# Four decoder layers on one core: loads into a ninth token tile, moved value-bias products and last norm, contiguous context parts, and a new order of both halves

## The reference, cut to what matters

```python
# L0: pre-norm
h = _mha(_ln(x), _ln(x), causal=True);  x = x + h @ m_proj_w + m_proj_b      # attention 0
h = _mha(_ln(x), ctx, causal=False);    x = x + h @ c_proj_w + c_proj_b      # attention 1
x = x + relu(_ln(x) @ f_w1 + f_b1) @ f_w2 + f_b2
# L1: post-norm, mixture of experts
x = _layernorm(x + _attn(x, x, x, causal=True))                              # attention 2
x = _layernorm(x + _attn(x, ctx, ctx, causal=False))                         # attention 3
x = _layernorm(x + _moe(x))      # 8 experts (256 to 1024 to 256, gelu), the best 2 of each token
# L2: post-norm
x = _ln(x + _mha(x, x, mask));  x = _ln(x + _mha(x, ctx, None))              # attentions 4, 5
x = _ln(x + relu(x @ ff_w1 + ff_b1) @ ff_w2 + ff_b2)
# L3
y = _ln(x + softmax(Q(x) K(ctx)^T / 4) V(ctx) @ Wo)                          # attention 6
```

## Time and profile before

| | |
|---|---|
| median of 3 runs | 3065.95 us (3065.38 to 3067.84) |
| the profiled execution | 3048.22 us |
| its span, first to last instruction | 3045.8 us |
| stage a, about | 0 to 1415 us |
| stage b, about | 1415 to 1950 us |
| stage c, about | 1950 us to the end |
| mean granted TensorE clock, share of full speed | 0.964 |

### The profile page before, as it was taken

How to read it: one execution, slowest core, us unless ns; L and a number is a source line. 1 busy time by engine, 2 the same in 40 slices (tenths; PEclk the granted TensorE clock), 3 DMA queues, 4 the chain that set the end, 5 groups by cost and what they waited for, 6 DMA issues and landing times. The chain is left out here.

```text
span 3045.8 us, 58500 instructions
## 1 busy us (share of the span) xinstructions
PE 2830.4 (93%) x22574; PEld 2279.3 (75%) x22574; DVE 1681.8 (55%) x4086; ACT 1331.7 (44%) x2955; POOL 986.7 (32%) x1103
## 2 busy tenths in 40 slices
PE   6989999989999989975999999889999999999996
PEld 4768888768888777754888888656777777777774
DVE  4646556776755867554110010276676766767664
ACT  2535445556455455332222222245455545555442
POOL 2313224444323444322000000252344444444343
PEclk8999999999999999986999999899999999999997
DMA  9755546585664674754767766375466555666342
GB/s 141 119 72 67 63 54 89 84 114 75 75 71 59 90 98 72 190 74 135 241 225 231 224 211 220 87 111 63 53 85 76 80 79 75 82 77 78 43 50 40
DMA packets 393627, 317.68 MB, mean 104 GB/s; under 512 B 152155, under 2 KB 377307, under 8 KB 393339
## 3 DMA queue, kind: packets, MB, share of 16 engines
q1 hardware_dynamic: 370994, 276.25, 54.6%
q0 software_dynamic: 8272, 23.73, 2.8%
q10 hardware_dynamic: 14085, 13.97, 1.7%
HBM read 133.54 MB, written 36.57 MB: 56 GB/s over the span
## 5 line engine op out<-in xcount | busy, mean ns | idle before, releaser
L962 ACT ACTIVATE a_prob<-a_bank 128x512 f32<-128x512 f32 (+1 forms) x640 | 332.8, 603 | 146.5 <-PE a_bank L756 142.9
L1106 DVE TENSOR_REDUCE a_maxima<-a_bank 128x2 f32<-128x512 f32 (+3 forms) x576 | 339.2, 644 | 82.7 <-PE a_bank L736 82.0
L962 ACT ACTIVATE c_prob<-c_bank 128x512 f32<-128x512 f32 (+1 forms) x512 | 266.3, 599 | 194.7 <-PE c_bank L756 194.4
L989 ACT ACTIVATE b_group_hidden<-b_bank,b_b 128x256 f32<-128x256 f32 (+1 forms) x312 | 123.3, 452 | 387.7 <-PE b_bank L820 387.7
L1106 DVE TENSOR_REDUCE c_maxima<-c_bank 128x6 f32<-128x462 f32 (+1 forms) x448 | 260.4, 635 | 45.2 <-PE c_bank L736 43.9
L865 PE MATMUL a_bank<-a_causal_b,keep_identb 128*128 128x256 bf16 (+1 forms) x768 | 243.1, 316 | 29.9 <-DMA a_qs<-a_shift 12.9
L820 PE MATMUL b_bank<-b_group_xt,b_w 128*128 128x256 f32 (+1 forms) x1248 | 261.6, 364 | 6.3 <-DVE b_group_xt L1157 6.3
L802 PE MATMUL b_bank<-b_w,b_group_hidden 128*128 128x256 f32 x1136 | 251.7, 380 | 0.9 <-ACT b_group_hidden L989 0.9
L820 PEld LDWEIGHTS b_bank<-b_group_xt,b_w 128*128 128x128 f32 x1248 | 220.6, 192 | 33.7 <-DVE b_group_xt L1157 8.3
L802 PEld LDWEIGHTS b_bank<-b_w,b_group_hidden 128*128 128x128 f32 x1136 | 215.6, 190 | 29.7 <-ACT b_group_hidden L989 1.3
L1163 DVE TENSOR_TENSOR b_group_y<-b_bank,b_b 128x512 f32<-128x512 f32 (+1 forms) x39 | 25.1, 644 | 336.1 <-PE b_bank L802 336.1
(11 more groups left out here) (255 smaller groups left out, 6224.0 us busy)
## 6 DMA issues: line engine op xcount, KB each, us to landing
b_w<-in_L_xattn_e_w SPq DMA_DIRECT2D x78, 1024.0 KB, 7.4
a_qs<-a_parts_q SPq DMA_DIRECT2D x384, 128.0 KB
c_qs<-c_parts_q SPq DMA_DIRECT2D x288, 128.0 KB
a_ks<-a_parts_k SPq DMA_DIRECT2D x192, 128.0 KB, 5.9
c_ks<-c_parts_k SPq DMA_DIRECT2D x96, 128.0 KB, 5.5
sorted_in<-a_zeros SPq DMA_DIRECT2D x8, 1024.0 KB
b_group_x<-sorted_in SPq DMA_DIRECT2D x32, 256.0 KB, 6.8
sorted_out<-b_group_y ACTq DMA_DIRECT2D x32, 256.0 KB, 4.8
```

Source lines behind the costliest of these rows:

```text
L962: act.activation(prob[0:rows, first:first + cols], bank[0:rows, 0, 0:cols], ACT.Exp, scale=SCALE).then_inc(k.own(s), 1)
L989: ins = act.activation(hidden[:, f, 0:n], bank[:, 0, j * n:(j + 1) * n], ACT.Gelu, bias=b1[:, f:f + 1])
L1106: v.tensor_reduce(maxima[:, q:q + qn, h:h + n].rearrange("p q h -> p h q"), bank[:, 0, 0:cols].rearrange("p (j q n) -> p j q n", j=n, q=qn ...
```

## The change

1. `enter` in stage a loads straight into a `tok` tile, which is the residual. `loaded` goes from stage a, and `tok` has 9 tiles. GpSimd's `bias` works in place after `apply`.
2. The value-bias products of stage a stand behind a step of sequence 0: product 0 behind its value projection of attention 0, products 1, 2 and 3 behind the first `pv` of attentions 0, 1 and 2.
3. The last norm of a sequence is two VectorE steps in place: `scaled` computes (x - mean) * gain after the moments, `shifted` computes x * rstd + shift. The two GpSimd passes and the `apply` go.
4. The context's input is laid out as [sequence, 128, 2, 77], so its load has one run per partition. Its three parts are packed at the front of their tile (`parts_of`), so that a copied part is one run of 308 bytes per partition, before two of 154.
5. The planner adds 0.1 us to the start of every TensorE step that leaves the 32-column products when it compares steps. Before, the 0.1 was added only once the choice was made.
6. Both tables of `AHEAD` have new numbers.
7. The router's small steps share one semaphore.

```diff
@@ class Plan, run
-                    start = max(free_at[e], came[k])
+                    leaves = e == "tensor" and in_columns and s.kind != "pv"
+                    start = max(free_at[e] + (0.1 if leaves else 0.0), came[k])
@@ semaphore_of
+        if s.kind in ROUTING:
+            return "routing"
@@
+def last_norm_steps(plan, b, n, x, source):
+    lab = (b, n)
+    moment_steps(plan, b, n, x, source)
+    plan.step("vector", "scaled", b, n, us=0.92, after=[("moments", b, n)], x=x, moments=("moments", lab))
+    plan.step("vector", "shifted", b, n, us=0.92, after=[("scaled", b, n), ("rstd", b, n)], gives=["moments", "rstd"],
+              x=x, moments=("moments", lab), rstd=("rstd", lab))
@@ value_bias_steps
-    plan.step("tensor", "bias_out", -1, "bias", at, us=0.87, after=ready, takes=["bank"], bank=bank)
+    plan.step("tensor", "bias_out", -1, "bias", at, us=0.87, after=ready, behind=behind, takes=["bank"], bank=bank)
@@ start_steps
-                         [("fold", -1, "a")] if at == 3 else [bias_in(at)])
+                         [("fold", -1, "a")] if at == 3 else [bias_in(at)], [("value_proj" if at == 0 else "pv", 0, max(at - 1, 0), 1 if at else 0)])
@@ AHEAD, the two first lines of each half
-AHEAD = {"a": {"enters": 0.9, ("enters", "a"): -0.6, "norms": 3.3, ("norms", 0): 126.0, ("gains", 0): -19.1,
-               "turns": -0.8, ("turns", 0): 2.0, "projs": 0.8, ("projs", 0): 13.1, "values": -0.4,
...
-         "c": {"enters": 2.3, "norms": 8.4, ("norms", 4): -9.6, "turns": 1.2, ("turns", 4): -0.2, "gains": 4.7,
-               ("gains", 4): 30.5, "projs": 0.7, ("projs", 4): -0.5, "values": -0.4, ("values", 4): 1.4,
...
+AHEAD = {"a": {"enters": -89.5, ("enters", "a"): 0.8, "norms": 3.2, ("norms", 0): 0.4, "gains": 7.4,
+               ("gains", 0): -29.7, "turns": -0.9, ("turns", 0): 45.1, "projs": 0.8, "values": -0.4,
...
+         "c": {"enters": 1.0, "norms": 19.2, ("norms", 4): 62.2, "turns": 1.2, ("turns", 4): 50.9, "gains": -41.9,
+               ("gains", 4): 5.4, "projs": 1.4, ("projs", 4): -1.9, "values": -0.5, ("values", 4): 1.5,
...
@@ first_half
-    x, res = ("loaded", b), ("tok", (b, "x"))
-    plan.step("sync", "enter", b, "a", us=0.45, lag=4.0, takes=["x", "lane"], landing="x", x=x, lane=("lane", (b, "a")))
-    norm_steps(plan, b, "l0_1", x, ("tok", (b, "n0")), ("enter", b, "a"), False)
-    bias_step(plan, b, 0, x, res, ("enter", b, "a"), after=[("apply", b, "l0_1")], takes=["out"], gives=["x"])
+    res = ("tok", (b, "x"))
+    plan.step("sync", "enter", b, "a", us=0.45, lag=4.0, takes=["x", "lane"], landing="x", x=res, lane=("lane", (b, "a")))
+    norm_steps(plan, b, "l0_1", res, ("tok", (b, "n0")), ("enter", b, "a"), False)
+    bias_step(plan, b, 0, res, res, ("apply", b, "l0_1"))
@@ second_half
-    z = ("tok", (b, "end"))
-    norm_steps(plan, b, "l3", q, z, ("add", b, 6), True)
-    gain_steps(plan, b, "l3", z)
+    last_norm_steps(plan, b, "l3", q, ("add", b, 6))
@@
+def parts_of(parts, role):
+    if role != "c":
+        return parts
+    return parts.rearrange("p a m t -> p (a m t)")[:, 0:NPART * KT * C].rearrange("p (a m t) -> p a m t", a=NPART, m=KT)
@@ vector_program
+        elif s.kind == "scaled":
+            for t in range(QT):
+                ins = v.scalar_tensor_tensor(x[:, t, :], x[:, t, :], moments[:, t, 0:1], k.gains[at][0], ALU.subtract, ALU.mult)
+        elif s.kind == "shifted":
+            for t in range(QT):
+                ins = v.scalar_tensor_tensor(x[:, t, :], x[:, t, :], rstd[:, 1, t:t + 1], k.gains[at][1], ALU.mult, ALU.add)
@@ sync_program
-            sp.dma_start(tile(s, "ctx"), k.ctx_in[b]).then_inc(k.own(s), 16)
+            sp.dma_start(tile(s, "ctx").rearrange("p k t -> p (k t)"), k.ctx_in[b].rearrange("p k t -> p (k t)")).then_inc(k.own(s), 16)
-                sp.dma_start(stack[block * HD:(block + 1) * HD, :, :], parts[:, part, :, 0:n]).then_inc(k.own(s), 16)
+                sp.dma_start(stack[block * HD:(block + 1) * HD, :, :], parts[:, part, :, :]).then_inc(k.own(s), 16)
@@ lane_pools
-    pool("tok", 8, [P, QT, D])
-    pool("loaded", 1 if name == "a" else 2, [P, QT, D])
+    pool("tok", 9 if name == "a" else 8, [P, QT, D])
+    if name == "c":
+        pool("loaded", 2, [P, QT, D])
@@ inputs
-              "ctx_t": v["ctx_1024"].reshape(B * C, D).T,
+              "ctx_t": v["ctx_1024"].reshape(B, C, KT, P).transpose(0, 3, 2, 1),
```

More of the change, by code:

```diff
@@ L62 @@
 Step = namedtuple("Step", "engine kind b at part us lag tiles takes gives after behind source landing transfers rank")
+ROUTING = ("logit", "logit_max", "logit_less", "route_sum", "route_recip", "route_prob", "top", "top_at", "gap", "chosen", "member", "row",
+           "run", "hit", "pair", "rows", "one_more", "share1", "share2", "table")
 class Plan:
@@ L242, in norm_steps, with moment_steps @@
     lab = (b, n)
+    moment_steps(plan, b, n, x, source)
+    plan.step("vector", "apply", b, n, us=0.76, after=[("rstd", b, n)], takes=["out"],
+              gives=["moments", "rstd"] + (["x"] if free_x else []),
+              x=x, out=out, moments=("moments", lab), rstd=("rstd", lab))
+def last_norm_steps(plan, b, n, x, source):
+    lab = (b, n)
+    moment_steps(plan, b, n, x, source)
+    plan.step("vector", "scaled", b, n, us=0.92, after=[("moments", b, n)], x=x, moments=("moments", lab))
+    plan.step("vector", "shifted", b, n, us=0.92, after=[("scaled", b, n), ("rstd", b, n)], gives=["moments", "rstd"],
+              x=x, moments=("moments", lab), rstd=("rstd", lab))
+def moment_steps(plan, b, n, x, source):
+    lab = (b, n)
     plan.step("vector", "stats", b, n, us=0.78, source=source, takes=["stats"], x=x, stats=("stats", lab))
@@ L248, in norm_steps @@
     plan.step("gpsimd", "rstd", b, n, us=0.71, lag=0.1, after=[("eps", b, n)], rstd=("rstd", lab))
-    plan.step("vector", "apply", b, n, us=0.76, after=[("rstd", b, n)], takes=["out"],
-              gives=["moments", "rstd"] + (["x"] if free_x else []),
-              x=x, out=out, moments=("moments", lab), rstd=("rstd", lab))
 def gain_steps(plan, b, n, x):
@@ L266, in turn_steps, with bias_step @@
     return ("xt", lab), ("turned", b, n)
-def bias_step(plan, b, at, x, out, source, after=(), takes=(), gives=()):
-    plan.step("gpsimd", "bias", b, at, us=1.27, lag=0.1, source=source, after=list(after) + [bias_in(at) if at == "l0_ff" else ("bias_fold", -1, "bias", at)], takes=takes, gives=gives,
+def bias_step(plan, b, at, x, out, source):
+    plan.step("gpsimd", "bias", b, at, us=1.27, lag=0.1, source=source, after=[bias_in(at) if at == "l0_ff" else ("bias_fold", -1, "bias", at)],
               x=x, out=out)
@@ L433, in start_steps @@
         value_bias_steps(plan, at, [("load", -1, "a", at), ("load", -1, "a", "first")],
-                         [("fold", -1, "a")] if at == 3 else [bias_in(at)])
-STAGES = {"enters": ("enter", "ctx_load"), "norms": ("stats", "moments", "eps", "rstd", "apply"), "turns": ("turn", "turned"),
+                         [("fold", -1, "a")] if at == 3 else [bias_in(at)], [("value_proj" if at == 0 else "pv", 0, max(at - 1, 0), 1 if at else 0)])
+STAGES = {"enters": ("enter", "ctx_load"), "norms": ("stats", "moments", "eps", "rstd", "apply", "scaled", "shifted"), "turns": ("turn", "turned"),
           "projs": ("proj", "high", "rest", "middle", "low", "copy"), "values": ("value_proj", "value"), "maxima": ("qm", "max"),
@@ L638, in second_half @@
     out_steps(plan, b, 6, heads, ("heads", b, 6), q, ("shift", b, "l2_3"), KT)
[L640 to L644 removed]
+    last_norm_steps(plan, b, "l3", q, ("add", b, 6))
+    plan.step("sync", "out_store", b, "c", us=0.45, lag=3.0, after=[("shifted", b, "l3")], gives=["x", "lane"], landing="x",
+              x=q, lane=("lane", (b, "c")))
 def expert_steps(plan, g):
@@ L940, in scalar_program @@
         elif s.kind == "high":
-            bank, parts, n = tile(s, "bank"), tile(s, "parts"), C if s.part == "c" else S
+            bank, parts, n = tile(s, "bank"), parts_of(tile(s, "parts"), s.part), C if s.part == "c" else S
             bias = k.biases[at][0 if s.part == "q" else 1]
@@ L948, in scalar_program @@
         elif s.kind == "middle":
-            parts, rest, n = tile(s, "parts"), tile(s, "rest"), C if s.part == "c" else S
+            parts, rest, n = parts_of(tile(s, "parts"), s.part), tile(s, "rest"), C if s.part == "c" else S
             until.wait_ge(*done("rest", b, at, s.part))
```

61 lines of the change are left out of this document (31 added, 30 removed).

## The result

The changed kernel takes 3099.29 us (8 runs, 3095.38 to 3105.70) beside 3069.93 us for the kernel before (8 runs, 3064.05 to 3085.62): ratio 1.0096, 95% interval 1.0081 to 1.0112. It is 1.0% slower, where 3034.7 us was forecast. The profiled execution took 3101.16 us, its span is 3099.4.

What follows compares the result with a forecast made beforehand. TensorE was taken as the bound, with 215.4 us idle. Terms summing to 31.3 us took the profiled 3048.22 to 3016.9; carrying over the runs' 17.7 gave 3034.7 us, range 3008 to 3058.

Steps and rivals of the forecast that it cites:

- the new order: All engines, both halves: new table numbers reorder the steps; counted at -4 us, bounds -23 and +15.
- The middle grows gaps that eat 20 us: Sign of failure: the middle of either half, then 2 to 5% idle, grows gaps that eat 20 us.
- The slower rival: First half: x loads ranked lowest on SP make the last sequence late, 45 us, giving 3080 us; chance 0.08.
- my sign of 1110: Sign of failure: the last load, issued at 1086.7 us before, is issued after 1110.
- Value-bias products: First half, TensorE: first turn 6.5 us earlier and a 7.3 us weight wait gone; -6.5 and -7.3 us.
- Residual tile: Stage a's start: x loads no longer wait for a tile, so turns wait less; -5 us, bounds 0 and -10.5.
- the 12.8 that I gave as a sign: Sign of success: TensorE idle about 16 us in the first 100 us, in place of 28.8.
- Grouping: TensorE's probability-value matmuls: fewer switches between kinds of matmul; -4 us, bounds 0 and -12.
- Last norm: Second half: -2.5 us at the end, and -1 us (bounds 0 and -3) from a lighter GpSimd.
- The rival that I gave 0.03: Last norm: the new VectorE instructions wait for GpSimd at the SBUF port, 18 us come back, 3053 us; chance 0.03.
- Contiguous context: Context copies and load in half as many pieces, same bytes; -1 us, bounds 0 and -5.
- Bytes weigh more than pieces: Context copies: landing time depends more on bytes than on pieces; 128 KB took 5.9 us, 38.5 KB took 3.3.

Runs made afterwards that it cites:

- e13: e5 run again on another chip: all parts of the change, first half in the order of before, second half planned anew with old numbers; 3032.23 us, ratio 0.9873.
- e14: e13 with the new numbers in its second half, so the order of the changed kernel there; 3053.71 us, ratio 0.9943.
- e15: e13 with the new numbers in its first half, so the order of the changed kernel there; 3075.31 us, ratio 1.0020.
- e1: Changed kernel with all its parts, but every engine runs the steps in the order of the kernel before; 3064.51 us, ratio 0.9991.
- e9: The kernel before, unchanged, run again on a third chip; 3073.50 us, ratio 0.9991.
- e10: The changed kernel, unchanged, run again on the same chip as e9; 3099.71 us, ratio 1.0074.
- e6: Changed kernel's order in the first half, but SP's loads free of it and ranked high; second half as in e5; 3059.74 us, ratio 1.0033.
- e5: All parts of the change, first half in the order of before, second half planned anew with the old numbers; 3014.70 us, ratio 0.9884.
- e8: e1 with the value-bias products back at their old places and both last-norm steps behind the root; 3068.68 us, ratio 1.0061.
- e12: e5 without the packed context, its layout as before; 3051.57 us, ratio 0.9924.
- e2: The kernel before with only the packed context parts and the context's new layout, order unchanged; 3045.20 us, ratio 0.9914.
- e11: e2 run again on the same chip as e9: the kernel before with the packed context only; 3060.88 us, ratio 0.9954.
- e7: Changed kernel with three first-half table numbers moved by 0.9 or less; only SP's list differs; 3094.51 us, ratio 1.0155.
- e4: Changed kernel with the two AHEAD tables of the kernel before; 3118.75 us, ratio 1.0164.

## Why the prediction was wrong, by its own steps

**The step that failed is the new order.** I counted it at -4 us and gave it bounds of -23 and +15. It costs some 65 us beside the best order measured for the same steps (e13 against e14 and e15): 43 to 48 in the first half, 20 to 22 in the second. The lower side of my argument was that the old order had been made for a stage with the `loaded` bottleneck. In the first half the runs showed the contrary: the order of before, imposed on the new steps, serves them well. In the second half it does not (1118.7 us in e1); there it is the old numbers, planned anew, that do (1084.8 in e13), and the new order lies between (1105.1 in e14). My upper bound took its size from the drain. The loss doesn't arise there: it lies in the middle, from 100 to 700 us, where the first half had been nearly full, and there more idle time came together with a lower granted clock, so that the same matmuls took longer too. "The middle grows gaps that eat 20 us" was one of my signs of failure, and it came.

**The slower rival: the length right, the cause wrong.** The last load of x did slip, from 1086.7 to 1133.9, over my sign of 1110, and the half ended 39 us later; on one chip (e9 to e10) the load slips by 27.2 and the half by 19.8, from e13 to e15 by 50.6 and 47.5. In every run looked at the half ends 333 to 344 us behind its last load, so that part of the rival held. But the rank is not what makes the load late. e6 gives the loads a high rank and still issues the last at 1116.5, where e5 does at 1068.6, and wins back only 7.7 us. A load needs a free lane, so it comes late when the sequences ahead of it do. The longest stall of a low-ranked load is that of the context at the start, 7.5 of 16.4 us.

**Value-bias products, -13.8: right.** e8 against e5 gives 14.4, one execution each; the first turn starts at 6.99 and L784's waits are gone.

**Residual tile, -5: not resolved.** Products and tile together give 17.3 us (e12 against e9) or 12.4 (e1 against e2) where I had 18.8. Less the products' 14.4 that leaves between -2 and 3 for the tile, and the numbers come from three chips. SP has no more waits at the x load, as I said. But the first 100 us lost 4.4 us of idle, not the 12.8 that I gave as a sign. In the order of after the context's load took 7.5 of them. In e13, in the order of before, TensorE is idle for 24.2 us there too, and the turns' waits for a norm, which I had at 10.5 and expected to halve, are 16.4.

**Grouping, -4: not seen.** The weight loads of the products (L788) have 103 idle moments by issue, where the earlier trace rows had 98 and I asked for under 85. The planner itself groups more in the first half (90 groups in place of 101) and not at all in the second, where all 96 steps stand alone in every plan. At 0.22 us a group that is at most 2.4 us. e5 and e13 have the 101 groups of before in their first half, so their gain owes nothing to it. No run isolated it.

**Last norm, -2.5 and -1: right where the half is planned anew.** 5.5 us in e12 against e9; the store follows the root by 1.0 us. GpSimd is busy 952.9 us and VectorE 1712.2, where I had 946 and 1700. The rival that I gave 0.03 is real in its rows: in the kernel after `scaled` takes 799 ns in the mean, in e1 `shifted` 1119. I had excluded it by L1171's mean of 510, a line whose neighbours on GpSimd are others. No run shows that it costs the kernel its 18 us. What cost 27 us (e1 against e2) was, by the waits, the place of the two steps before the maxima's steps, a price that my sum did not have.

**Contiguous context, -1: right in sign, mis-sized.** 12 to 26 us. "Bytes weigh more than pieces" compared a copy of 128 KB with one of 38.5 and so could not tell what half the pieces would do. The row of the kernel after can:

```profile
a_ctx_ks<-a_parts_k SPq DMA_DIRECT2D x192, 38.5 KB, 2.2
```

2.2 us in place of 3.3, and 2.6 in e2 and e11, where the order is that of before: a fifth to a third less for the first half's 192 copies of unchanged bytes. The packets fell from 393627 to 336283, and from e9 to e11 the DMA share of the first half from 0.60 to 0.57. The waits for `qs` hardly moved: 25.0 us for `c_shift` in e9 and 22.4 in e11. How the shorter copies and loads become 12 to 26 us is open.

**Without the order term** my sum would have been 27.3. The parts measured give 17.3 + 5.5 + 12 to 26, so 35 to 49 (30 to 44 with the 12.4 of e1); e5 and e13 show 35.1 and 36.9. With the order's 65 against it, 36.9 makes the kernel after 28 us slower than before; it is 29.4 slower by the medians. The order's term was off by some 69 us (65 in place of -4), and the other parts, some 10 us better than my 27.3, hid that much of it.

**What stays open** is why the planner does not see the loss. Its own ends differ by 1.8 us for the two orders of the first half (1331.7 and 1333.5) and by 0.9 for the second (1056.3 and 1057.2), the chip's by 47.5 and 20.3. It reckons with fixed times for a copy to land and with one clock. That both fall short where copies crowd fits the waits above, but no run varied either. Which engine's list in the new order does the harm is open too: e6 and e7 bound only the place of the loads on SP, by 7.7 us. The change's point 7, the shared semaphore, is in every run with the new parts and was not taken apart.

## What to carry to other kernels

Take an order that is fitted to a model's landing times as a change of its own, and time it half by half against the old order imposed on the new steps and against the old numbers planned anew: here two orders that the model holds to be 1.8 us apart are 47.5 apart. A table of priorities can lose much on other steps than those it was tuned on (36 and 90 us in the first half), and it can also win (e4's second half), so it has to be timed. And when a step moves from GpSimd to VectorE, look at who waits behind it there before looking at its own duration: the same two steps at another place cost 27 us.

## What the runs showed of the hardware that I had not expected

- Copies between SBUF tiles of 256 pieces of 154 B landed in 3.3 us in the median, of 128 pieces of 308 B in 2.2 to 2.8. The kernel gained 0.4 to 0.9%, with the context's loads going from pieces of 308 B to 616 B at the same time.
- A VectorE instruction with two SBUF inputs took 475 to 485 ns in the kernel after (`shifted`), and in e1 1382 in the median of 32, of which 22 started beside a GpSimd pass; the worst took 1491 there and 1512 in e8 (`scaled`). Beside it GpSimd's small `eps` step took 0.51 us in place of 0.22.
- The same kernel took 3050, 3067, 3069 and 3076 us on four chips, 0.9% from end to end, nearly as much as the whole change.
